# Moving picks, columns, a norm and some distances between slots and from VectorE to GpSimd in a fused convolution, attention and expert kernel

## What is computed

```
px = ww + deform[..., 0];  py = hh + deform[..., 1]
x0, y0 = floor(px), floor(py);  wx1, wy1 = px - x0, py - y0
samp = gather(y0, x0) * wy0 * wx0 + ... + gather(y0 + 1, x0 + 1) * wy1 * wx1
out  = einsum('bhwgkc,bhwgk->bhwgc', samp, weights)
```

## Time and profile before

| | |
|---|---|
| median of three runs | 1269.87 us (1262.55 to 1270.61) |
| profiled execution | 1256.5 us |
| its span, first to last instruction | 1254.8 us |
| mean granted clock of PE | 0.903 of full speed |
| busy: PE, DVE, ACT, POOL | 970.8, 828.5, 785.5, 661.5 us |
| chain that ended last: PE, ACT, DVE, POOL | 53%, 19%, 16%, 3% |

### The profile page before, as it was taken

How to read it: one execution, slowest core, us unless ns; L and a number is a source line. 1 busy time by engine, 2 the same in 40 slices (tenths; PEclk the granted TensorE clock), 3 DMA queues, 4 the chain that set the end, 5 groups by cost and what they waited for, 6 DMA issues and landing times.

```text
span 1254.8 us, 50908 instructions
## 1 busy us (share of the span) xinstructions
PE 970.8 (77%) x22310; PEld 792.0 (63%) x22310; DVE 828.5 (66%) x1556; ACT 785.5 (63%) x1474; POOL 661.5 (53%) x627
## 2 busy tenths in 40 slices
PE   4477785877679776899788768997897767687974
PEld 3465664666547665787467656887476656467974
DVE  4876857676766876556766875667767758546444
ACT  2676774667566755786677675666767557345652
POOL 2665543465545567443666585444666675102374
PEclk9699797988889888999899788999998779898997
DMA  7803130132000133373111313553111330543713
GB/s 160 173 25 59 49 74 24 59 57 85 25 7 26 36 105 100 92 209 111 47 40 36 93 52 89 160 162 104 39 38 32 106 93 20 153 135 113 208 50 97
DMA packets 142782, 104.80 MB, mean 84 GB/s; under 512 B 43698, under 2 KB 125939, under 8 KB 142051
## 3 DMA queue, kind: packets, MB, share of 16 engines
q1 hardware_dynamic: 138242, 92.68, 26.9%
q0 software_dynamic: 4320, 8.86, 2.3%
HBM read 76.32 MB, written 25.19 MB: 81 GB/s over the span
## 4 chain that ended last, share of the span: by engine, by line
PE 53%; ACT 19%; DVE 16%; issue 6%; POOL 3%; DMA 2%; SPq 0%; DVEq 0%; POOLq 0%; ACTq 0%
PE ps L1043 14%; PE ps L1027 9%; ACT xsb L1419 7%; PE ps L1270 7%; PE ps L1283 6%; PE ps L1051 5%; DVE asb L1786 4%; ACT asb L1437 2%; ACT xsb L1413 2%; DVE ysb L1777 2%; ACT osp L1428 2%; PE ps L983 2%; PE ps L1163 2%; PE ps L1165 1%; PE ps L1202 1%
## 5 line engine op out<-in xcount | busy, mean ns | idle before, releaser
L900 POOL TENSOR_TENSOR ysb<-ysb,rw 128x576 f32<-128x576 f32 x300 | 338.9, 1151 | 333.4 <-DVE ysb L1777 332.9
L1027 PE MATMUL ps<-xsb,ysb 64*64 64x96 f32 x11008 | 324.6, 268 | 105.8 <-DVE asb L1786 35.7
L1027 PEld LDWEIGHTS ps<-xsb,ysb 64*64 64x64 f32 x11008 | 275.3, 148 | 165.7 <-issue 80.2
L1419 ACT ACTIVATE xsb<-xsb,pick 128x576 f32<-128x576 f32 (+1 forms) x480 | 337.7, 752 | 5.2
L1786 DVE COPY asb<-ps 128x960 f32<-128x960 f32 (+1 forms) x208 | 216.6, 1045 | 110.9 <-PE ps L1043 102.9
L1043 PE MATMUL ps<-asb,vd 32*32 32x258 f32 x8192 | 182.3, 388 | 17.5 <-issue 9.1
L1428 ACT ACTIVATE osp<-ps 128x258 f32<-128x258 f32 x128 | 43.0, 444 | 238.3 <-PE ps L1043 238.3
L889 POOL TENSOR_TENSOR ysb<-rw,count 128x576 f32<-128x576 f32 (+1 forms) x122 | 140.6, 1153 | 72.3 <-PE ps L1027 71.9
L1043 PEld LDWEIGHTS ps<-asb,vd 32*32 32x32 f32 x8192 | 123.0, 103 | 66.4 <-issue 34.2
L1511 ACT ACTIVATE region<-ps,b_col 128x128 f32<-128x128 f32 x368 | 105.3, 371 | 70.8 <-PE ps L1270 70.5
L1751 DVE TENSOR_TENSOR xsb<-rw,ps 128x576 f32<-128x576 f32 (+1 forms) x150 | 108.3, 722 | 47.1 <-PE ps L1027 45.2
(11 more groups left out here) (311 smaller groups left out, 1215.7 us busy)
## 6 DMA issues: line engine op xcount, KB each, us to landing
ring<-in_L_ffn_W SPq DMA_DIRECT2D x122, 256.0 KB, 3.3
vd<-group_values SPq DMA_DIRECT2D x128, 128.0 KB, 2.6
set_rows<-ring SPq DMA_DIRECT2D x4, 1376.0 KB, 6.3
rw<-set_rows SPq DMA_DIRECT2D x30, 172.0 KB, 3.8
group_values<-region SPq DMA_DIRECT2D x32, 128.0 KB, 3.5
asb<-in_L_ffn_W SPq DMA_DIRECT2D x16, 256.0 KB, 5.5
region<-sorted_rows SPq DMA_DIRECT2D x6, 512.0 KB, 5.2
expert_rows<-region SPq DMA_DIRECT2D x6, 512.0 KB
```

What stands on the lines that cost most here:

```text
L900: pl.tensor_tensor(ysb[:, ch % DEPTH, 0:sets, u, :], ysb[:, ch % DEPTH, 0:sets, NU - 1, :], rows_of(ig)[:, 2 + u, first:first + sets].rear ...
L1027: last = pe.matmul(ps[64 * j:64 * j + 64, bank + i, NV * GRID * q:NV * GRID * (q + 1)], ysb[rows, ch % DEPTH, col, :, :].rearrange("p u y ...
L1419: act.activation(xsb[:, ch % DEPTH, 0:sets, v, :], xsb[:, ch % DEPTH, 0:sets, NV - 1, :], ACT.Relu, bias=pick[:, v:v + 1], scale=-1.0).the ...
```

## The change

It has four parts, none of which changes what is computed.

1. For images 0 to 2, `centre_rows` on POOL, in slot 7, makes the norm in two operations on the whole tile (subtract the mean, multiply by the reciprocal) and adds the bias in a third. DVE keeps the reciprocal. `std` moves from slot 7 to 6, `turn_tn` and `tnT` from 9 to 10, `temps` from 11 to 12, `recip0` from 12 to 13. Image 3 keeps its places.
2. For ten chunks per stage (issued at the even slots 14 to 32) POOL makes the x distances, behind the y distances and ahead of `weigh`. A second semaphore counts them, and those who wait for x distances wait for both.
3. The columns' steps of images 0 to 2 move to slots 49, 51 and 53.
4. The picks of images 0 and 1 move to slots 57 to 71, one in a slot and two in slot 71; their adds to slots 72 to 78, two or three in a slot. The number of slots of the adds also holds for image 2 in the tail, whose first add keeps its place.

```diff
-PE_STEPS = {9: ("turn_tn",), 11: ("temps",), 16: ("logits0",), ...
+PE_STEPS = {10: ("turn_tn",), 12: ("temps",), 16: ("logits0",), ...
-ACT_STEPS = {7: ("std",), 9: ("tnT",), 16: ("logits0",), ...
+ACT_STEPS = {6: ("std",), 10: ("tnT",), 16: ("logits0",), ...
-DVE_STEPS = {3: ("stats",), 7: ("normalise",), 8: ("bout",), 11: ("temps",), 12: ("recip0",), 14: ("recip1",),
+DVE_STEPS = {3: ("stats",), 7: ("normalise",), 12: ("temps",), 13: ("recip0",), 14: ("recip1",),
...
-             44: ("columns0",), 45: ("b2",), 46: ("columns1",), 47: ("columns2",)}
+             45: ("b2",), 49: ("columns0",), 51: ("columns1",), 53: ("columns2",)}
...
+CENTRE_SLOT, NORMAL_SLOT = 7, 38
...
-PICK_SLOT, PICK_SLOTS = 89, 24
-ADD_SLOT, ADD_SLOTS = 143, 15
+PICK_SLOT, PICK_SLOTS = 137, 15
+ADD_SLOT, ADD_SLOTS = 152, 7
...
+def x_by_pool(ch):
+    return ch >= 3 and 14 <= 2 * (ch - 3) % SLOTS < 34
...
+        def wait_x(eng, chunks):
+            eng.wait_ge(s.x_away, chunks - X_APART[chunks])
+            if X_APART[chunks]:
+                eng.wait_ge(s.x_apart, X_APART[chunks])
...
+            def centre_rows(b):
+                pl.wait_ge(s.values_stored, 16 * G * B)
+                pl.wait_ge(s.rows_stored, 16 * B)
+                pl.wait_ge(s.ln_recip, b + 1)
+                if b:
+                    pl.wait_ge(s.xn_ready, b)
+                x1 = image(b)
+                pl.tensor_tensor(tn_tok, x1, f_mv[:, :, 0:1].broadcast_to([P, NT, C]), ALU.subtract).then_inc(s.centred, 1)
+                pl.wait_ge(s.centred, b + 1)
+                pl.tensor_tensor(tn_tok, tn_tok, f_r[:, :].rearrange("p (t o) -> p t o", o=1).broadcast_to([P, NT, C]),
+                                 ALU.mult).then_inc(s.tile_normalised, 1)
+                pl.tensor_tensor(x1, x1, boutb_b[:, :].rearrange("p (o c) -> p o c", o=1).broadcast_to([P, NT, C]),
+                                 ALU.add).then_inc(s.bout_added, 1)
...
+            def x_distances(ch):
+                ig, first, sets = chunk_of(ch)
+                pl.tensor_tensor(xsb[:, ch % DEPTH, 0:sets, NV - 1, :],
+                                 rows_of(ig)[:, 0, first:first + sets].rearrange("p (s o) -> p s o", o=1)
+                                 .broadcast_to([P, sets, GRID]),
+                                 count[:, :].rearrange("p (o q) -> p o q", o=1).broadcast_to([P, sets, GRID]),
+                                 ALU.subtract).then_inc(s.x_apart, 1)
...
                         y_distances(ch + 3)
+                        if x_by_pool(ch + 3):
+                            x_distances(ch + 3)
...
-                    chain(s.ln_recip, dve.reciprocal(f_r[:, :], f_sd[:, :]), b + 1)
+                    dve.reciprocal(f_r[:, :], f_sd[:, :]).then_inc(s.ln_recip, 1)
+                    if b < B - 1:
+                        return
+                    dve.wait_ge(s.ln_recip, b + 1)
...
-                        x_distances(ch + 3, grid_of(bank))
+                        if not x_by_pool(ch + 3):
+                            x_distances(ch + 3, grid_of(bank))
```

More of the change, by code:

```diff
@@ L72 @@
 TURN_SLOT, JOIN_SLOT = 10, 12
-PE_STEPS = {9: ("turn_tn",), 11: ("temps",), 16: ("logits0",), 17: ("logits1",), 18: ("logits2",), 19: ("logits3",),
+PE_STEPS = {10: ("turn_tn",), 12: ("temps",), 16: ("logits0",), 17: ("logits1",), 18: ("logits2",), 19: ("logits3",),
             21: ("turn_e0",), 23: ("turn_e1",), 25: ("sums",), 26: ("eid",), 27: ("M",), 28: ("out",),
@@ L77 @@
             43: ("ranks",), 44: ("turn_gate",), 45: ("b2",)}
-ACT_STEPS = {7: ("std",), 9: ("tnT",), 16: ("logits0",), 17: ("logits1",), 18: ("logits2",), 19: ("logits3", "exp0"),
+ACT_STEPS = {6: ("std",), 10: ("tnT",), 16: ("logits0",), 17: ("logits1",), 18: ("logits2",), 19: ("logits3", "exp0"),
              21: ("e0", "exp1"), 23: ("e1",), 25: ("sums",), 27: ("M",),
              31: ("std1",), 33: ("std2",), 35: ("xt",), 38: ("exp",), 42: ("xn",), 44: ("gateT",)}
-DVE_STEPS = {3: ("stats",), 7: ("normalise",), 8: ("bout",), 11: ("temps",), 12: ("recip0",), 14: ("recip1",),
+DVE_STEPS = {3: ("stats",), 7: ("normalise",), 12: ("temps",), 13: ("recip0",), 14: ("recip1",),
              16: ("logits0",), 17: ("logits1", "max0"), 18: ("logits2",), 19: ("logits3", "max1"),
@@ L84 @@
              32: ("normalise1",), 36: ("second", "top"), 40: ("gates",), 43: ("rows",),
-             44: ("columns0",), 45: ("b2",), 46: ("columns1",), 47: ("columns2",)}
-ACT_LAST = {**ACT_STEPS, 5: ("std",), 7: (), 15: ("warm",), 20: ("exp1",), 19: ("logits3", "exp0"), 21: ("e0",)}
-DVE_LAST = {**DVE_STEPS, 6: ("normalise",), 7: (), 12: ("recip0", "recip1"), 14: (), 34: ("second", "normalise2"), 36: ("top",)}
-NORMAL_SLOT = 38
+             45: ("b2",), 49: ("columns0",), 51: ("columns1",), 53: ("columns2",)}
+ACT_LAST = {**ACT_STEPS, 5: ("std",), 6: (), 15: ("warm",), 20: ("exp1",), 19: ("logits3", "exp0"), 21: ("e0",)}
+DVE_LAST = {**DVE_STEPS, 44: ("columns0",), 46: ("columns1",), 47: ("columns2",), 49: (), 51: (), 53: (),
+            6: ("normalise",), 7: (), 8: ("bout",), 12: ("temps", "recip0", "recip1"), 13: (), 14: (), 34: ("second", "normalise2"), 36: ("top",)}
+CENTRE_SLOT, NORMAL_SLOT = 7, 38
 WEIGHT_SLOT = 45
@@ L116 @@
 rows_even rows_odd values_even values_odd
-x_away x_within x_ready y_apart y_away y_within y_ready a_summed a_taken a_lifted out_summed out_copied
+x_away x_apart x_within x_ready y_apart y_away y_within y_ready a_summed a_taken a_lifted out_summed out_copied
 projected half_projected half_added conv_added
-ln_chain ln_stats ln_std ln_recip tile_normalised tn_turned tnT_copied
+ln_chain ln_stats ln_std ln_recip centred tile_normalised tn_turned tnT_copied
 temps_summed scale_chain rtemp_ready bout_added logits_summed logits_biased logits_done
@@ L142, in apart @@
     return ch >= 3 and 44 <= 2 * (ch - 3) % SLOTS < 58
+def x_by_pool(ch):
+    return ch >= 3 and 14 <= 2 * (ch - 3) % SLOTS < 34
+X_APART = [0]
+for _ch in range(ALL_CHUNKS):
+    X_APART.append(X_APART[-1] + x_by_pool(_ch))
 APART = [0]
@@ L621, in load_rows_of @@
                 if ig >= 4:
-                    sp.wait_ge(s.x_away, len(CHUNK_SETS) * (ig - 1))
+                    wait_x(sp, len(CHUNK_SETS) * (ig - 1))
                     sp.wait_ge(s.y_ready, NU * len(CHUNK_SETS) * (ig - 1))
@@ L869, in side @@
                 for b_, at in (works(b, slot) if b < B else tail_works(slot)):
+                    if at == CENTRE_SLOT and b_ < B - 1:
+                        centre_rows(b_)
                     if at == NORMAL_SLOT and b_ < B - 1:
@@ L1387, in prepare @@
                     if b == 1 and h == 0:
-                        act.wait_ge(s.x_away, 2 * len(CHUNK_SETS))
+                        wait_x(act, 2 * len(CHUNK_SETS))
                         act.wait_ge(s.y_ready, 2 * NU * len(CHUNK_SETS))
@@ L1409, in x_edges @@
             def x_edges(ch):
-                act.wait_ge(s.x_away, ch + 1)
+                wait_x(act, ch + 1)
                 away = xsb[:, ch % DEPTH, 0:chunk_of(ch)[2], NV - 1, :]
```

## The result

The changed kernel took 1284.43 us, the median of four runs (1280.47 to 1287.78), against 1267.14 for four of the kernel before: 1.0136 times as long, with a 95% interval of 1.0091 to 1.0180. Forecast were 1284 us and 14.7 us of loss; the medians differ by 17.3. The two profiled executions differ by 24.0 (1280.47 and 1256.5), since the one of before is 10.6 under its median and the one of the change 4.0. The sum of the forecast is met, but several of its terms are not, as will be seen.

A forecast was written before the change was run, and what follows sets the result against it. No relieved engine was taken as the bound; whichever wait ends last sets each slot. Terms 9.0, 1.5, 0.4, 1.5, 0.3, 0.8 and 1.2 sum to +14.7 us over 1269.87, giving 1284 us; range 1266 to 1294.

The forecast's parts named there:

- The picks in stage 3: Stage 3, slots 57 to 79: POOL's full queue lands the last pick late, DVE stands 7.4 us; +9.0 us.
- Stage 2's adds: Stage 2, slot 75: a triple of adds ahead of a copy TensorE waits for, no stall for picks; +1.5 us.
- The norm: Stages 1 to 3: POOL's norm ready about as before, temperature's operations about 1.5 us later; +0.5 each, +1.5 us.
- The x distances: Stage 0: five pieces leave DVE's chain, POOL's instructions lengthen DVE's SBUF operations, the two cancelling; +0.3 us.
- terms 3 and 4: x distances on POOL, +0.3 us, and picks out of slots 9 to 32 with x distances coming in, +0.8 us.
- Picks out of slots 9 to 32: Stage 2 regains about 1.0 us; x distances in the same slots cost 1.8 over three stages; net +0.8 us.
- The columns: Slots 49, 51, 53 of stages 1 to 3: second piece delays a ramp, +0.4 each, +1.2 us.
- The tail: Image 2's first add becomes a pair ahead of the copy that ends TensorE's idle time; +0.4 us.
- B: Rival: no stall for picks at stage 3's end, +7.3 us in all, 1277 us; chance 0.2.
- C: Rival: DVE's relief shows in slots 7 to 12 of stages 1 to 3, -3.7 us each, 1272 us; chance 0.12.
- D: Rival: POOL's new operations hold DVE's SBUF operations at the ports, +20.7 us, 1295 to 1305 us; chance 0.1.
- E: Rival: picks or adds not where the tables say, images 0 and 1 run as now, 1268 to 1272 us; chance 0.03.

The follow-up runs named there:

- experiment 1: Kernel before with only the picks moved to slots 57 to 71 and the adds to 72 to 78; ratio 1.0070 to the kernel before.
- experiment 2: Kernel before with only the adds moved to slots 72 to 78, picks left in slots 9 to 32; ratio 1.0005 to the kernel before.
- experiment 3: Kernel before with norm and bias on POOL and std, turn, temps, recip0 one slot later; ratio 1.0058 to the kernel before.
- experiment 7: Kernel before with only the x distances of ten chunks per stage on POOL; ratio 1.0052 to the kernel before.
- experiment 9: Kernel before with only the columns' steps of images 0 to 2 moved to slots 49, 51, 53; ratio 0.9967 to the kernel before.
- experiment 6: POOL norm with later steps, plus the first logits' first product made three times ahead of the temperatures' wait; ratio 0.9964 to the kernel before.

## Why the prediction held, point by point

- **The picks in stage 3** (forecast +9.0, measured +10.5 and, alone, +10.6). The mechanism is shown by experiments 1 and 2, and its parts came out near: 5.80 for 5.96 a chunk, the first add 6.7 us later than before for 7.4. The form of the wait was off. I had DVE standing once, 7.4 us (5 to 9 as the sign); it stood 2.44 in stage 3 and 2.33 in stage 2. In stage 3 that is because the late weighings, which I called hidden in the stall, delayed DVE's own way to slot 72 by the rest. Of the 1.5 us over, 1.6 come from adds that take longer while POOL weighs and 0.7 from slot 79's product at the lower clock, less the 0.7 by which the first add came sooner.
- **Stage 2's adds** (+1.5; measured 3.1, in experiment 1 1.7, in experiment 2 2.5). The triple in slot 75 cost 1.66, as argued. The picks also landed 2.3 us after DVE came for them, which I had denied; the products of slots 72 and 73 lost no more than 0.8 us by it.
- **The norm** (+1.5; measured alone +7.3 by medians, 3.5 to 11.1). This is the step that failed. POOL's two operations took 1.91 and 1.90, as priced by the row of 1.92, and the logits' start behind slot 15's product moved from 1.66 to 3.27 us, near the 1.5 that I had. But I took that 1.5 as the whole price of the temperature's later slot, less what the earlier contraction gives. What it did to TensorE's clock was not asked: the exchanges behind the gap ran at 0.50, 5.57 us instead of 3.68 each, and filling the gap took the time from 1.0058 to 0.9964. That was left out though the earlier trace rows had a window at 0.84 in plain view. Its range of -2 to +2 a stage did not hold stages 1 and 2 of experiment 3 (+5.4 and +6.5).
- **The x distances** (+0.3) took 1.12 to 1.17 each on POOL, as priced; they read `count` there instead of the grid in PSUM (no POOL instruction of these traces reads PSUM). In the whole change stage 0 is +0.1; experiment 7 shows that with picks beside them they do cost, so the parts aren't additive: terms 3 and 4 of the forecast hang together, and no experiment has their sum alone.
- **Picks out of slots 9 to 32** (+0.8). The gain in stage 2 was 0.8 in slots 26 and 27, for the 1.0 forecast; the half instruction that I charged for x distances there doesn't show: `a_norm` took 0.73. I also misread the 2.94: the pick that I counted had ended at 652.30, before `a_norm` began at 652.58, and the y distance and the two weighings alone held it, to 655.49. By the rule of the Trainium skill named in the forecast, SBUF — State Buffer, section "SBUF: two separate sides", a blocked operation waits out whole POOL instructions: 4.02 behind four agrees with it.
- **The columns** (+1.2): the delay that I priced at 0.4 a stage is there, at 0.6 in slots 50 to 59 (experiment 9). But I put at nothing what the slots give back that the columns leave, and that is 1.1 a stage (both by comparing profiles, not by an experiment of their own); alone the ratio is at or below 1.
- **The tail** (+0.4): -1.7 in the one profile, +0.1 in that of experiment 1, so no finding.

So the total of 14.7 was near in part by luck. The largest term was right with its mechanism. The norm's was too small by about 6 us, and the columns', at +1.2, stands against -4.2 measured alone (-8.5 to 0), which offsets most of it. The ratios of experiments 1, 3 and 9 multiply to 1.0095; the 5 us that are left to 1.0136 are within the intervals, and I can't assign them.

Of the rivals, B (no stall) is refuted by experiment 1. C (DVE's relief shows in slots 7 to 12) is refuted by 3; in the change TensorE's transposes start at 599.25 in stage 2's terms of before, not ahead of 596. D (the ports) has its mechanism in experiment 7, but at a place where the whole change mostly avoids it. E is refuted by the picks in POOL's timeline.

## What to carry to other kernels

Before steps are moved, count each queue's instructions over the slots where they go: POOL had 339 us of room in the run, but 11.9 us in the ten slots that mattered, where the eleven picks needed 14. Where one wait at the head of a batch covers the whole batch, the last of it sets the time, and everything behind that wait on the engine moves with it. And when a step before a long run of products moves later, ask what the gap does to TensorE's clock: it may cost several times the gap, and a product made early and repeated can buy it back, as in experiment 6.

## What the hardware showed that I had not expected

- TensorE's granted clock fell in 28 of 30 stages in which the waits around slot 15 were left, in the kernel before too. In 8 of them it stayed low for most of slots 16 to 19, which then took up to 18 us with TensorE busy nearly all the time; in the others it was full again at the latest 4.0 us after the beginning of slot 16's product. Two of the 8 are in kernels whose steps there were not moved.
- An operation on 256 elements took between 0.16 and 4.02 us, by what POOL happened to have in its queue.
- At the end of stage 3 TensorE ran its product of slot 79 in 1.56 us and the projection in 3.16, against 0.89 and 1.98 before. All three kernels with the picks moved have the 1.56, but so have four of the others, so that the stall brings the lower clock isn't shown.
